# Graph attention layer on one core: the row's largest score kept as one more column of the score tile, both low halves of P written in one VectorE pass, variance plus epsilon on GpSimd

## The chip, the core and the metric

One Trainium2 chip, one of its cores. The metric is the device time of one execution in microseconds (us). Short names as in the profile: PE is TensorE (PEld its weight loads), DVE is VectorE, ACT is ScalarE, POOL is GpSimd, SP is SyncE.

## The reference

`x` is (8, 2048, 256) in f32, `adj` is (8, 2048, 2048) in int32 with about one entry in 512 set, `W` is 256 x 256, `a` has 512 entries.

```python
h = jnp.maximum(_layernorm(x, axis=-1), 0.0)
Wh = jnp.einsum('bnf,fo->bno', h, W)
f1 = Wh @ a[:fout, 0];  f2 = Wh @ a[fout:, 0]
e = f1[:, :, None] + f2[:, None, :]
e = jnp.where(e >= 0, e, ALPHA * e)
attention = jnp.where(adj > 0, e, MASK_FILL)
attention = jax.nn.softmax(attention, axis=1)
h_prime = jnp.einsum('bij,bjo->bio', attention, Wh)
out = x + jax.nn.elu(h_prime)
```

The softmax runs over the rows i. So the kernel holds P transposed: a tile has 128 columns j of the attention on its partitions and all 2048 rows i along the free axis, and a row of that tile is one softmax.

## The kernel before

The work is cut into 128 chunks, 16 for each of the 8 batches; a chunk is 128 nodes j. Each engine has its own program, written out by hand as a loop over steps s, and the programs meet at semaphores. In step s the engines work on these chunks:

- PE: the product h W of chunk s+17 (`make_wh`, L365); `store_block(s-9)`, 24 matmuls for a 128-row block of the upper half of i over the 8 chunks of a group (L435 to L437); `transpose_mask(s+1)`, 16 transposes that put the mask into PSUM (L387); `transpose_x(s+18)` (L377); `direct_blocks(s-1)`, 16 matmuls with the high part of P (L453, L455) and, behind a wait for the low part, 8 with it (L460).
- ACT: `take_f` and `split_v_high` for chunk s+17 (L508, L512), `attention(s)` (L519 to L530), `make_h(s+18)` (L542), at times `keep_part` (L558) and `finish_relu` (L575), `normalise(s+19)` (L548), at times `finish_exp` (L579), and `split_high_stored(s)` (L536), which waits for POOL's 1/total (`inv`).
- DVE: `mask_scores(s)` (L696) adds mask and f1 and takes the largest score of each row in the same pass; `statistics` and `aggregate` of chunk s+23 (L661, L666); every fourth step `add_eps` (L672); `split_v_low(s+17)` (L702); `split_low(s-1)`, two passes of 1024 columns (L710 for the half that is used directly, L715 for the stored half); every fourth step `make_offset` (L677); `make_mask(s+2)` (L684); at times `finish_elu` (L731) and `add_halves` (L726).
- POOL: `split_high(s-1)` (L802, L805, L808); at times the DMA of `finish_add` (L828); every second step the mask load (L794); every fourth step `root`, which makes 1/sqrt(variance + epsilon) of four chunks (L815).

P is written as the sum of two f16 tiles, high and low, for a matmul at f16 speed that keeps more bits; the low one is P minus the high one. `attention(s)` is a chain: Prelu of the largest score (L519, 128x1), Prelu of the score tile (L521, 128x2048), the negated largest as the shift (L523), Exp with that shift as its bias (L530).

The steps with a `root`, called root steps below, are s = 0, 4, 8, ..., 104 (five more lie before step 0). In a root step DVE's order is: scores, statistics, add_eps, v_low, the two low passes, offset, mask, elu, halves, and then the scores of the next step. `make_offset` waits for `root`; everything behind it on DVE waits too, the scores of the next step among it, which ACT's `attention` needs.

Of the kernel before, what the change touches and what calls it, by code (L numbers as in the profile page):

```python
# [13 lines left out]
P = 128  # L14
ALPHA = 0.2
# [6 lines left out]
def graph_attention(nc, x, adj, W, a, out):  # L22
# [27 lines left out]
    with ExitStack() as ctx:  # L50
# [34 lines left out]
        spare = stored[:, 1].rearrange("p g h c -> p (g h c)").bitcast(F32).rearrange("p (i c) -> p i c", c=F)  # L85
# [10 lines left out]
        top = sb("top", [P, R], F32)  # L96
        most = sb("most", [P, R], F32)
# [40 lines left out]
        most_s = sem("most_s")  # L138
# [7 lines left out]
        lo_direct = sem("lo_direct")  # L146
        lo_stored = sem("lo_stored")
# [32 lines left out]
        def f2_col(c):  # L180
            return 64 + c % RF

# [173 lines left out]
        def _(pe):  # L356
# [58 lines left out]
            def store_block(n):  # L415
                group, q = divmod(n, G)
                pe.wait_ge(lo_stored, G * (group + 1))
# [13 lines left out]
                for c in range(G):  # L431
                    p_st = stored[:, group % 2, c]
                    v_c = v[:, (G * group + c) % RV]
                    rows = slice(q * P, (q + 1) * P)
                    nc.tensor.matmul(bank[:, 0:FO], p_st[:, 0, rows], v_c[:, 0, :], start=(c == 0), stop=False)  # L435
                    nc.tensor.matmul(bank[:, 0:FO], p_st[:, 0, rows], v_c[:, 1, :], start=False, stop=False)  # L436
                    last = nc.tensor.matmul(bank[:, 0:FO], p_st[:, 1, rows], v_c[:, 0, :], start=False,  # L437
                                            stop=(c == G - 1))
                last.then_inc(stored_done, 1)

            def direct_blocks(c):
# [5 lines left out]
                p_d = direct[:, c % 2]  # L447
                v_c = v[:, c % RV]
                for m in range(NB):
# [3 lines left out]
                    nc.tensor.matmul(acc[:, m, :], p_d[:, 0, rows], v_c[:, 0, :],  # L453
                                     start=(j == 0 and m % 2 == 0), stop=False, skip_group_check=True)
                    nc.tensor.matmul(acc[:, m, :], p_d[:, 0, rows], v_c[:, 1, :],  # L455
                                     start=False, stop=False, skip_group_check=True)
                pe.wait_ge(lo_direct, c + 1)
                for m in range(NB):
                    rows = slice(m * P, (m + 1) * P)
                    last = nc.tensor.matmul(acc[:, m, :], p_d[:, 1, rows], v_c[:, 0, :],  # L460
# [32 lines left out]
        def _(act):  # L493
# [20 lines left out]
            def attention(c):  # L514
                b, j = divmod(c, C)
                act.wait_ge(scores, c + 1)
                p = prob[:, c % 2, :]
# [9 lines left out]
                act.wait_ge(leaky, c + 1)  # L527
# [5 lines left out]
            def split_high_stored(c):  # L533
                act.wait_ge(inv_ready, c + 1)
                wait(act, stored_done, G * (c // G - 1))
                nc.scalar.activation(stored[:, c // G % 2, c % G, 0, :], prob[:, c % 2, HALF:N], ACT.Copy,  # L536
# [79 lines left out]
        def _(dve):  # L616
# [70 lines left out]
            def mask_scores(c):  # L687
# [4 lines left out]
                if c == 0:  # L692
                    dve.wait_ge(f1_last, 1)
                wait(dve, lo_stored, c - 1)
                wait(dve, most_s, c - R + 1)
                nc.vector.tensor_tensor_reduce(  # L696
                    out=prob[:, c % 2, :], in0=tp_b, in1=f1_row[:, b % 2, :], scale=1.0, scalar=-3.0e38,
                    op0=ALU.add, op1=ALU.max, accum_out=top[:, c % R:c % R + 1]).then_inc(scores, 1)
# [6 lines left out]
            def split_low(c):  # L705
                p = prob[:, c % 2, :]
# [27 lines left out]
            for s in range(FIRST, END + 2):  # L734
                if chunk(s):
                    mask_scores(s)
                for c in measured_at(s):
                    statistics(c)
                    aggregate(c)
                    if c % 4 == 3:  # L740
                        add_eps(c // 4)
# [123 lines left out]
```

## Time and profile before

| | |
|---|---|
| median of 3 runs | 1006.8 us (1006.44 to 1007.97) |
| profiled execution: its time, its span | 1006.23 us, 1004.4 us |
| busy share of the span: PE, ACT, DVE, POOL | 95%, 93%, 87%, 54% |
| granted TensorE clock, mean | 0.997 |
| a batch of 16 chunks, first scores to first scores (503.12 to 621.96) | 118.8 us, that is 7.4 us a step |

A busy share sums the spans of instructions. On ACT and DVE the next instruction starts about 0.1 us before the one in front has ended, so times of a sequence are read from start to start.

### The profile page before, as it was taken

The page shows a single profiled execution, that of the slowest core. Times are in us where ns is not written, and L with a number is a line of the kernel's source. Part 1 is how long each engine was busy: PE and PEld are TensorE (multiplying, and loading weights), DVE is VectorE, ACT ScalarE, POOL GpSimd, SP SyncE. Part 2 cuts the span into 40 slices and gives each one's busy share as a digit, 9 for nine tenths or more (in the row PEclk, how much of TensorE's full clock was granted, in tenths as well). Part 3 has the DMA queues.
Part 4 walks back from the last instruction along what each step waited for, and adds up shares of the span by engine and source line. Part 5 has one row for each costly group of instructions (what it writes and reads, how often), then busy time and mean ns, then how long its engine had stood idle before and what let it go on. Part 6 is the DMA issues. An engine that isn't in the chain of part 4 may idle for free. (4 is left out here: it accounts for less than half of the span.)

```text
span 1004.4 us, 23981 instructions
## 1 busy us (share of the span) xinstructions
PE 958.5 (95%) x8988; PEld 835.2 (83%) x8988; DVE 875.3 (87%) x1261; ACT 929.5 (93%) x1472; POOL 544.0 (54%) x574
## 2 busy tenths in 40 slices
PE   8878999999999999999999999999999999999996
PEld 6656888898888888888888888888888888888886
DVE  7799988999899998899988998899988988798763
ACT  3799999999999999999999999999999999998983
POOL 5445543655545655655556565465565554555534
PEclk9999999999999999999999999999999999999999
DMA  9577657889969978888978987888996987889535
GB/s 222 89 100 116 99 100 119 153 152 161 165 115 164 166 141 157 134 160 158 168 132 137 168 156 148 140 152 152 160 168 114 163 148 125 160 116 147 96 73 168
DMA packets 199061, 142.13 MB, mean 142 GB/s; under 512 B 7329, under 2 KB 187809, under 8 KB 198946
## 3 DMA queue, kind: packets, MB, share of 16 engines
q0 software_dynamic: 140160, 81.80, 60.4%
q1 hardware_dynamic: 58786, 58.81, 19.6%
q8 instruction: 72, 1.18, 0.5%
q14 instruction: 43, 0.35, 0.1%
HBM read 176.16 MB, written 16.84 MB: 192 GB/s over the span
## 5 line engine op out<-in xcount | busy, mean ns | idle before, releaser
L696 DVE CUSTOM_DVE_ANT_0 prob<-tp,f_row 128x2048 f32<-128x2048 bf16 x128 | 292.1, 2282 | 10.5 <-DMA f_row<-f_scratch 10.5
L435 PE MATMUL acc_st<-v,stored 128*128 128x256 f16 x992 | 270.2, 272 | 9.2 <-ACT part L558 5.1
L437 PE MATMUL acc_st<-v,stored 128*128 128x256 f16 x992 | 270.3, 273 | 0.0
L436 PE MATMUL acc_st<-v,stored 128*128 128x256 f16 x992 | 270.3, 272 | 0.0
L530 ACT ACTIVATE prob<-prob,shift 128x2048 f32<-128x2048 f32 x128 | 256.5, 2004 | 9.9
L521 ACT ACTIVATE prob<-prob,f 128x2048 f32<-128x2048 f32 x128 | 255.6, 1997 | 0.0
L808 POOL TENSOR_TENSOR direct<-prob,inv 128x1024 f16<-128x1024 f32 x128 | 242.4, 1894 | 10.0
L802 POOL TENSOR_SCALAR small_total<-total 128x1 f32<-128x1 f32 x128 | 28.7, 224 | 401.9 <-ACT prob L530 401.9
L453 PE MATMUL acc<-v,direct 128*128 128x256 f16 x1024 | 231.4, 273 | 4.8 <-ACT z_direct L564 4.8
L455 PE MATMUL acc<-v,direct 128*128 128x256 f16 x1024 | 231.3, 273 | 0.0
L710 DVE SCALAR_TENSOR_TENSOR direct<-prob,inv,direct 128x1024 f16<-128x1024 f32 x128 | 163.1, 1274 | 23.3 <-POOL direct L808 22.3
L715 DVE SCALAR_TENSOR_TENSOR stored<-prob,inv,stored 128x1024 f16<-128x1024 f32 x128 | 163.6, 1278 | 0.0
L536 ACT ACTIVATE stored<-prob,inv 128x1024 f16<-128x1024 f32 x128 | 146.2, 1142 | 17.0 <-POOL inv L805 17.0
L387 PE MATMUL tp<-ident_b,neg 128*128 128x128 bf16 x2048 | 136.1, 220 | 1.9 <-DVE top L696 1.1
L365 PE MATMUL pre<-w_cat,h_t 128*128 128x258 f32 x444 | 120.9, 394 | 14.7 <-ACT h_t L542 14.6
L460 PE MATMUL acc<-v,direct 128*128 128x256 f16 x1024 | 132.7, 273 | 0.0
L387 PEld LDWEIGHTS tp<-ident_b,neg 128*128 128x128 bf16 x2048 | 125.3, 98 | 7.8 <-issue 5.1
L435 PEld LDWEIGHTS acc_st<-v,stored 128*128 128x128 f16 x992 | 96.8, 98 | 27.6 <-issue 14.9
L436 PEld LDWEIGHTS acc_st<-v,stored 128*128 128x128 f16 x992 | 96.9, 98 | 21.5
L453 PEld LDWEIGHTS acc<-v,direct 128*128 128x128 f16 x1024 | 100.3, 98 | 16.9 <-ACT z_direct L564 6.7
L455 PEld LDWEIGHTS acc<-v,direct 128*128 128x128 f16 x1024 | 100.3, 98 | 11.5
L460 PEld LDWEIGHTS acc<-v,direct 128*128 128x128 f16 x1024 | 100.2, 98 | 11.6
(85 smaller groups left out, 1344.6 us busy)
## 6 DMA issues: line engine op xcount, KB each, us to landing
raw<-in_adj POOLq DMA_DIRECT2D x64, 1024.0 KB, 10.0
y<-in_x SPq DMA_DIRECT2D x64, 256.0 KB, 2.9
out<-y SPq DMA_DIRECT2D x64, 256.0 KB, 2.2
y<-elu POOLq DMA_DIRECT2D x56, 256.0 KB, 4.3
x_in<-in_x SPq DMA_DIRECT2D x108, 128.0 KB, 3.7
f_row<-f_scratch SPq DMA_DIRECT2D x31, 256.0 KB, 6.4
stored<-in_x SPq DMA_DIRECT2D x4, 512.0 KB, 5.9
f_scratch<-f_t SPq DMA_DIRECT2D x124, 0.5 KB
```

The lines of the kernel that those rows point to most:

```text
L387: last = nc.tensor.transpose(tp_b[:, m * P:(m + 1) * P], neg[:, c % 2, m, :], ident_b[:])
L435: nc.tensor.matmul(bank[:, 0:FO], p_st[:, 0, rows], v_c[:, 0, :], start=(c == 0), stop=False)
L436: nc.tensor.matmul(bank[:, 0:FO], p_st[:, 0, rows], v_c[:, 1, :], start=False, stop=False)
L437: last = nc.tensor.matmul(bank[:, 0:FO], p_st[:, 1, rows], v_c[:, 0, :], start=False, stop=(c == G - 1))
L453: nc.tensor.matmul(acc[:, m, :], p_d[:, 0, rows], v_c[:, 0, :], start=(j == 0 and m % 2 == 0), stop=False, skip_group_check=True)
L455: nc.tensor.matmul(acc[:, m, :], p_d[:, 0, rows], v_c[:, 1, :], start=False, stop=False, skip_group_check=True)
L460: last = nc.tensor.matmul(acc[:, m, :], p_d[:, 1, rows], v_c[:, 0, :], start=False, stop=(j == C - 1), skip_group_check=True)
L521: nc.scalar.activation(p, p, ACT.Prelu, bias=f2, alpha=ALPHA).then_inc(leaky, 1)
L530: nc.scalar.activation(p, p, ACT.Exp, bias=shift[:, c % R:c % R + 1], accum_out=total[:, c % R:c % R + 1]).then_inc(prob_ready, 1)
L696: nc.vector.tensor_tensor_reduce(out=prob[:, c % 2, :], in0=tp_b, in1=f1_row[:, b % 2, :], scale=1.0, scalar=-3.0e38, op0=ALU.add, op1=ALU ...
L715: nc.vector.scalar_tensor_tensor(out=st[:, 1, :], in0=p[:, HALF:N], scalar=k, in1=st[:, 0, :], op0=ALU.mult, op1=ALU.subtract).then_inc(lo ...
L808: nc.gpsimd.tensor_tensor(direct[:, c % 2, 0, :], p[:, 0:HALF], k.to_broadcast([P, HALF]), ALU.mult).then_inc(hi_direct, 1)
```

## The change

1. `prob` gets two more columns. `mask_scores` writes the largest score into column 2048 of the score tile, and one Prelu of 2049 columns takes the place of the Prelu of the largest score and that of the tile. The shift now waits for that large Prelu (semaphore `leaky`) and reads its last column.
2. The tiles `direct` and `stored` become slots of one tile `split`, laid out so that the two low halves of a chunk are a pair of slots with a constant step between them. `split_low` is one pass of 128x2x1024, which waits for both high halves and signals `lo_ready`; both readers on PE wait for that.
3. `add_eps` leaves DVE. Its `tensor_scalar` is issued by POOL in `root`, in front of the power.

```diff
-        prob = sb("prob", [P, 2, N], F32)
-        direct = sb("direct", [P, 2, 2, HALF], F16)
-        stored = sb("stored", [P, 2, G, 2, HALF], F16)
+        prob = sb("prob", [P, 2, N + 2], F32)
+        split = sb("split", [P, 4 + 4 * G, HALF], F16)
...
+        def direct_slot(c, low):
+            return (10, 0)[c % 2] + low
+
+        def stored_slot(c, low):
+            return ((12, 2), (28, 20))[c // G % 2][c % 2] + 2 * (c % G // 2) + low
...
-                pe.wait_ge(lo_direct, c + 1)
+                pe.wait_ge(lo_ready, c + 1)
...
-                nc.scalar.activation(most[:, c % R:c % R + 1], top[:, c % R:c % R + 1], ACT.Prelu, bias=f2, alpha=ALPHA
-                                     ).then_inc(most_s, 1)
-                nc.scalar.activation(p, p, ACT.Prelu, bias=f2, alpha=ALPHA).then_inc(leaky, 1)
-                act.wait_ge(most_s, c + 1)
-                nc.scalar.activation(shift[:, c % R:c % R + 1], most[:, c % R:c % R + 1], ACT.Copy, scale=-1.0
+                nc.scalar.activation(p_top, p_top, ACT.Prelu, bias=f2, alpha=ALPHA).then_inc(leaky, 1)
+                act.wait_ge(leaky, c + 1)
+                nc.scalar.activation(shift[:, c % R:c % R + 1], prob[:, c % 2, N:N + 1], ACT.Copy, scale=-1.0
                                      ).then_inc(shift_s, 1)
...
-            def add_eps(g):
-                dve.wait_ge(mv_s, 4 * g + 4)
-                wait(dve, rstd_s, g - RS // 4 + 1)
-                rs = slice(4 * g % RS, 4 * g % RS + 4)
-                nc.vector.tensor_scalar(var_eps[:, rs], mv[:, rs, 1], EPS, None, ALU.add).then_inc(var_s, 1)
...
-                    op0=ALU.add, op1=ALU.max, accum_out=top[:, c % R:c % R + 1]).then_inc(scores, 1)
+                    op0=ALU.add, op1=ALU.max, accum_out=prob[:, c % 2, N:N + 1]).then_inc(scores, 1)
...
                 dve.wait_ge(hi_direct, c + 1)
+                dve.wait_ge(hi_stored, c + 1)
                 wait(dve, direct_done, c - 1)
-                nc.vector.scalar_tensor_tensor(out=direct[:, c % 2, 1, :], in0=p[:, 0:HALF], scalar=k,
-                                               in1=direct[:, c % 2, 0, :], op0=ALU.mult, op1=ALU.subtract
-                                               ).then_inc(lo_direct, 1)
-                dve.wait_ge(hi_stored, c + 1)
-                st = stored[:, c // G % 2, c % G]
-                nc.vector.scalar_tensor_tensor(out=st[:, 1, :], in0=p[:, HALF:N], scalar=k, in1=st[:, 0, :],
-                                               op0=ALU.mult, op1=ALU.subtract).then_inc(lo_stored, 1)
+                nc.vector.scalar_tensor_tensor(
+                    out=split[:, lo_d:lo_s + 1:lo_s - lo_d, :], in0=prob[:, c % 2, 0:N].rearrange("p (h c) -> p h c", h=2),
+                    scalar=inv[:, c % R:c % R + 1], in1=split[:, hi_d:hi_s + 1:hi_s - hi_d, :],
+                    op0=ALU.mult, op1=ALU.subtract).then_inc(lo_ready, 1)
...
             def root(g):
+                rs = slice(4 * g % RS, 4 * g % RS + 4)
+                pool.wait_ge(mv_s, 4 * g + 4)
+                wait(pool, xn_ready, 4 * g + 4 - RS)
+                nc.gpsimd.tensor_scalar(var_eps[:, rs], mv[:, rs, 1], EPS, None, ALU.add).then_inc(var_s, 1)
                 pool.wait_ge(var_s, g + 1)
-                wait(pool, xn_ready, 4 * g + 4 - RS)
-                rs = slice(4 * g % RS, 4 * g % RS + 4)
                 nc.gpsimd.tensor_tensor(rstd[:, rs], var_eps[:, rs], minus_half[:], ALU.pow).then_inc(rstd_s, 1)
```

DVE in root step 72, before, from the statistics on:

```order
L661 BN_STATS stats<-x_in 128x6 [waits mv_s,x_in_s3]
L666 BN_AGGR mv<-stats 128x2 [waits xn_ready,stats_s]
L672 TENSOR_SCALAR var_eps<-mv 128x4 [waits rstd_s,mv_s]
L702 TENSOR_TENSOR v<-pre,v 128x256 [waits v_hi]
L710 SCALAR_TENSOR_TENSOR direct<-prob,inv,direct 128x1024 [waits direct_done,hi_direct]
L715 SCALAR_TENSOR_TENSOR stored<-prob,inv,stored 128x1024 [waits hi_stored]
L677 SCALAR_TENSOR_TENSOR offset<-mv,rstd 128x4 [waits rstd_s]
L684 TENSOR_SCALAR neg<-raw 128x2048 [waits tp_ready,raw_in1]
```

The same place of the changed kernel:

```order
L662 BN_STATS stats<-x_in 128x6 [waits mv_s,x_in_s3]
L667 BN_AGGR mv<-stats 128x2 [waits xn_ready,stats_s]
L696 TENSOR_TENSOR v<-pre,v 128x256 [waits v_hi]
L705 SCALAR_TENSOR_TENSOR split<-prob,inv,split 128x2x1024 [waits direct_done,hi_stored,hi_direct]
L672 SCALAR_TENSOR_TENSOR offset<-mv,rstd 128x4 [waits rstd_s]
L679 TENSOR_SCALAR neg<-raw 128x2048 [waits tp_ready,raw_in1]
```

The variance row is gone and one pass stands where two stood; between the v row and the offset DVE has one instruction of twice the size.

POOL in the same step, before, with the first row of the next step:

```order
L805 TENSOR_TENSOR inv<-small_total,minus_one 128x1 [waits lo_stored,total_s]
L808 TENSOR_TENSOR direct<-prob,inv 128x1024 [waits direct_done,inv_ready]
L794 DMA raw<-in_adj 128x16x256 [waits neg_ready]
L815 TENSOR_TENSOR rstd<-var_eps,minus_half 128x4 [waits xn_ready,var_s]
L802 TENSOR_SCALAR small_total<-total 128x1 [waits prob_ready]
```

The same place of the changed kernel:

```order
L795 TENSOR_TENSOR inv<-small_total,minus_one 128x1 [waits lo_ready,total_s]
L798 TENSOR_TENSOR split<-prob,inv 128x1024 [waits direct_done,inv_ready]
L784 DMA raw<-in_adj 128x16x256 [waits neg_ready]
L805 TENSOR_SCALAR var_eps<-mv 128x4 [waits xn_ready,mv_s]
L807 TENSOR_TENSOR rstd<-var_eps,minus_half 128x4 [waits var_s]
L792 TENSOR_SCALAR small_total<-total 128x1 [waits prob_ready]
```

The variance row now stands behind the mask load's DMA issue and ahead of the power, which waits for it.

## Rows read from the trace of the kernel before

**Rows 1.** Busy time of the engines in one stretch (windows): PE, PEld, DVE, ACT, POOL.

```profile
540.00:660.00 120.00, 118.65 (x1130) 104.31 (x1128) 109.04 (x158) 116.82 (x187) 67.67 (x69) 1.00 0.86 151
```

**Rows 2.** Waits of the whole execution: total us, times, longest us.

```profile
ACT stored L536 <- POOL inv L805: 17.0, 42, 1.0
PE pre L365 <- ACT h_t L542: 14.6, 22, 2.9
ACT most L519 <- DVE top L696: 6.5, 11, 0.7
```

**Rows 3.** Timeline of ACT, step 72 into step 73: start us, duration us, instruction.

```profile
566.48 0.30 ACT L519 ACTIVATE most<-top,f 128x1 f32<-128x1 f32 x1
566.68 1.99 ACT L521 ACTIVATE prob<-prob,f 128x2048 f32<-128x2048 f32 x1
568.58 0.20 ACT L523 ACTIVATE shift<-most 128x1 f32<-128x1 f32 x1
568.85 2.00 ACT L530 ACTIVATE prob<-prob,shift 128x2048 f32<-128x2048 f32 x1
...
573.34 0.29 ACT L519 ACTIVATE most<-top,f 128x1 f32<-128x1 f32 x1
```

**Rows 4.** Timeline of ACT in step 117: the second waits for the first.

```profile
901.78 0.61 ACT L575 ACTIVATE elu<-z_st 128x512 f32<-128x512 f32 x1
902.42 0.63 ACT L579 ACTIVATE elu<-elu 128x512 f32<-128x512 f32 x1
```

**Rows 5.** Groups of instructions by line.

```profile
L805 POOL TENSOR_TENSOR inv<-small_total,minus_one 128x1 f32<-128x1 f32 x128 | 74.6, 583 | 10.8
...
L460 PE MATMUL acc<-v,direct 128*128 128x256 f16 x1024 | 132.7, 273 | 0.0
```

**Rows 6.** Timeline of DVE, root step 72 to the scores of chunk 73.

```profile
566.96 1.28 DVE L710 SCALAR_TENSOR_TENSOR direct<-prob,inv,direct 128x1024 f16<-128x1024 f32 x1
568.15 1.28 DVE L715 SCALAR_TENSOR_TENSOR stored<-prob,inv,stored 128x1024 f16<-128x1024 f32 x1
569.35 0.15 DVE L677 SCALAR_TENSOR_TENSOR offset<-mv,rstd 128x4 f32<-128x4 f32 x1
...
571.02 2.28 DVE L696 CUSTOM_DVE_ANT_0 prob<-tp,f_row 128x2048 f32<-128x2048 bf16 x1
```

**Rows 7.** Timelines of POOL and DVE: the power of root steps 72, 32 and 68.

```profile
567.62 1.53 POOL L815 TENSOR_TENSOR rstd<-var_eps,minus_half 128x4 f32<-128x4 f32 x1
...
268.67 1.05 POOL L815 TENSOR_TENSOR rstd<-var_eps,minus_half 128x4 f32<-128x4 f32 x1 [0.45 <-DVE var_eps L672]
268.82 1.27 DVE L710 SCALAR_TENSOR_TENSOR direct<-prob,inv,direct 128x1024 f16<-128x1024 f32 x1
...
538.35 1.28 DVE L715 SCALAR_TENSOR_TENSOR stored<-prob,inv,stored 128x1024 f16<-128x1024 f32 x1
538.40 2.13 POOL L815 TENSOR_TENSOR rstd<-var_eps,minus_half 128x4 f32<-128x4 f32 x1
540.56 0.16 DVE L677 SCALAR_TENSOR_TENSOR offset<-mv,rstd 128x4 f32<-128x4 f32 x1 [0.94 <-POOL rstd L815]
```

**Rows 8.** Timelines of DVE and POOL, end of root step 68: elu pass, small power.

```profile
541.23 0.23 POOL L802 TENSOR_SCALAR small_total<-total 128x1 f32<-128x1 f32 x1 [0.70 <-ACT prob L530]
541.25 0.70 DVE L731 SCALAR_TENSOR_TENSOR elu<-elu,z_st 128x512 f32<-128x512 f32 x1
541.54 0.84 POOL L805 TENSOR_TENSOR inv<-small_total,minus_one 128x1 f32<-128x1 f32 x1
```

**Rows 9.** Timelines of DVE and ACT: end of the scores, start of attention; steps 65 and 77.

```profile
512.54 0.08 DVE L696 DVE_READ_ACCUMULATOR2_ANT top<- 128x1 f32 x1
514.01 0.32 ACT L519 ACTIVATE most<-top,f 128x1 f32<-128x1 f32 x1
...
602.27 0.08 DVE L696 DVE_READ_ACCUMULATOR2_ANT top<- 128x1 f32 x1
602.75 0.31 ACT L519 ACTIVATE most<-top,f 128x1 f32<-128x1 f32 x1
```

More of the change, by code:

```diff
@@ L431, in store_block @@
                 for c in range(G):
-                    p_st = stored[:, group % 2, c]
+                    p_hi = split[:, stored_slot(G * group + c, 0), :]
+                    p_lo = split[:, stored_slot(G * group + c, 1), :]
                     v_c = v[:, (G * group + c) % RV]
                     rows = slice(q * P, (q + 1) * P)
-                    nc.tensor.matmul(bank[:, 0:FO], p_st[:, 0, rows], v_c[:, 0, :], start=(c == 0), stop=False)
-                    nc.tensor.matmul(bank[:, 0:FO], p_st[:, 0, rows], v_c[:, 1, :], start=False, stop=False)
-                    last = nc.tensor.matmul(bank[:, 0:FO], p_st[:, 1, rows], v_c[:, 0, :], start=False,
+                    nc.tensor.matmul(bank[:, 0:FO], p_hi[:, rows], v_c[:, 0, :], start=(c == 0), stop=False)
+                    nc.tensor.matmul(bank[:, 0:FO], p_hi[:, rows], v_c[:, 1, :], start=False, stop=False)
+                    last = nc.tensor.matmul(bank[:, 0:FO], p_lo[:, rows], v_c[:, 0, :], start=False,
                                             stop=(c == G - 1))
@@ L446, in direct_blocks @@
                     pe.wait_ge(f_ready, LEAD)
-                p_d = direct[:, c % 2]
+                p_hi, p_lo = split[:, direct_slot(c, 0), :], split[:, direct_slot(c, 1), :]
                 v_c = v[:, c % RV]
@@ L452, in direct_blocks @@
                     rows = slice(m * P, (m + 1) * P)
[L453 removed]
+                    nc.tensor.matmul(acc[:, m, :], p_hi[:, rows], v_c[:, 0, :],
                                      start=(j == 0 and m % 2 == 0), stop=False, skip_group_check=True)
[L455 removed]
+                    nc.tensor.matmul(acc[:, m, :], p_hi[:, rows], v_c[:, 1, :],
                                      start=False, stop=False, skip_group_check=True)
[L457 removed]
+                pe.wait_ge(lo_ready, c + 1)
                 for m in range(NB):
                     rows = slice(m * P, (m + 1) * P)
[L460 removed]
+                    last = nc.tensor.matmul(acc[:, m, :], p_lo[:, rows], v_c[:, 0, :],
                                             start=False, stop=(j == C - 1), skip_group_check=True)
@@ L535, in split_high_stored @@
                 wait(act, stored_done, G * (c // G - 1))
-                nc.scalar.activation(stored[:, c // G % 2, c % G, 0, :], prob[:, c % 2, HALF:N], ACT.Copy,
+                nc.scalar.activation(split[:, stored_slot(c, 0), :], prob[:, c % 2, HALF:N], ACT.Copy,
                                      scale=inv[:, c % R:c % R + 1]).then_inc(hi_stored, 1)
@@ L693, in mask_scores @@
                     dve.wait_ge(f1_last, 1)
-                wait(dve, lo_stored, c - 1)
-                wait(dve, most_s, c - R + 1)
+                wait(dve, lo_ready, c - 1)
                 nc.vector.tensor_tensor_reduce(
-                    out=prob[:, c % 2, :], in0=tp_b, in1=f1_row[:, b % 2, :], scale=1.0, scalar=-3.0e38,
-                    op0=ALU.add, op1=ALU.max, accum_out=top[:, c % R:c % R + 1]).then_inc(scores, 1)
+                    out=prob[:, c % 2, 0:N], in0=tp_b, in1=f1_row[:, b % 2, :], scale=1.0, scalar=-3.0e38,
+                    op0=ALU.add, op1=ALU.max, accum_out=prob[:, c % 2, N:N + 1]).then_inc(scores, 1)
             def split_v_low(c):
@@ L803, in split_high @@
                 pool.wait_ge(total_s, c + 1)
-                wait(pool, lo_stored, c - R + 1)
+                wait(pool, lo_ready, c - R + 1)
                 nc.gpsimd.tensor_tensor(k, t, minus_one[:], ALU.pow).then_inc(inv_ready, 1)
```

23 lines of the change are left out of this document (8 added, 15 removed).

## Prediction, made before the changed kernel ran

> **What bounds the kernel now.** I read the windows first. In a stretch of 120 us in the middle PE is busy for 118.65 us and ACT for 116.82, DVE for 109.04 and POOL for 67.67 [rows 1]. By busy time PE would be the bound and ACT a close second; the shares can't decide it, so the list of waits comes next. It has PE waiting for ACT's h_t at L365 (14.6 us in 22 waits), ACT waiting for POOL's `inv` at L536 (17.0 us, 42 waits) and ACT waiting for DVE's scores at L519 (6.5 us, 11 waits) [rows 2]. In the steady part I find no row where ACT waits for PE. So PE follows ACT, and ACT sets the pace: by its own work, by a loop through POOL (Exp, total, `inv`, L536), and at some steps by the scores. The wait for `inv` is a latency that ACT itself starts, so it shortens with nothing here. The wait for the scores is the one to look at, because the change touches what is queued ahead of the scores on DVE.
>
> The timelines say how near DVE is to being late. In step 73 the scores start at 571.02 and last 2.28 us [rows 6]; they end at 573.30, and ACT starts chunk 73 at 573.34 [rows 3]. The list counts no wait there, but there is no slack either. In step 77 the scores have ended at 602.35 and ACT starts at 602.75: 0.40 us. In step 65 it is 512.62 and 514.01: 1.39 us [rows 9]. As a start 0.03 us behind a release is what an engine needs at best (below), the slacks are 0, 0.37 and 1.36 us. These three, with step 69, follow a root step, and from batch 1 on they recur every 16 chunks: 6 steps like 69, 6 like 73, 6 like 65, and 5 like 77, since the last root step is 104.
>
> **The change part by part.** *ACT, attention.* Before, the small Prelu starts at 566.48 and Exp at 568.85: 2.37 us [rows 3]. After, the large Prelu starts where the small one did and takes 1.99 us (one column more is nothing), then the shift waits for it. What such a wait costs is shown by relu and exp of elu in the tail, where the second waits for the first: 901.78 + 0.61 = 902.39, start at 902.42, a gap of 0.03 [rows 4]. Then the shift, 0.20, and the gap to Exp, 0.07 as now (568.78 to 568.85). Sum 1.99 + 0.03 + 0.20 + 0.07 = 2.29, so 0.08 us saved; I take 0.07. Bounds: with a gap of 0.07 behind the large Prelu too, 0.03 to 0.04; with 0.03 at both places, 0.12. So the removed instruction is mostly not won: its issue was 0.20 us, and the overlap of the shift with the Prelu's end is lost. The saving counts only where ACT's own chain decides. 17 of the 128 chunks lie in the waits priced below, and I leave out ten more for the two ends. 100 x 0.07 = **7.0 us won** (3 to 11).
>
> *DVE, one low pass.* The two passes start 1.19 and end their turn 1.20 us later: 568.15 - 566.96 and 569.35 - 568.15, together 2.39 [rows 6]. No pass of this form and 2048 columns is in the trace. The score pass with as many columns takes 2.28 us, or 2.20 to the next start if the overlap is 0.08 as for the low pass (1.28 against 1.20). Between 2.20 and 2.39 I take 2.25: 0.14 us less. On DVE that is off the path except where DVE is what ACT waits for. The direct low half is ready about 1 us later than now. PE has 16 high-part matmuls in front of the low ones, and in the whole execution no idle time ahead of L460 [rows 5], so I cost it at nothing in the steady part; in the last chunk it may lie bare, at most one half pass, and I leave it out.
>
> *add_eps to POOL.* DVE loses a small instruction whose successor, v_low, waits for ACT's v anyway in most steps: nothing on the path. POOL gets one, 0.23 us as its 128x1 row has, and 0.08 to the next (541.23 + 0.23 to 541.54) [rows 8]: 0.31 us ahead of the power in each root step. Behind the power on POOL is the next chunk's total; behind `make_offset` on DVE are mask, elu, halves and the next scores.
>
> *The two together.* This is the term that decides. The same power (128x4) takes 1.53, 1.05 and 2.13 us [rows 7], and the lengths have a pattern. In step 32 it starts at 268.67, before the first low pass (268.82), and takes 1.05. In step 72 it starts at 567.62, inside the first pass; its end less 1.05 is 569.15 - 1.05 = 568.10, just where the second pass starts (568.15) [rows 6, 7]. In step 68 it starts at 538.40, just inside the second pass, and its end less 1.05 is 539.48; that pass ends at 538.35 + 1.20 = 539.55. So POOL's power seems to stand still until a low pass is over and to slip in at the seam between two. The small power shows the same beside the elu pass: 0.84 us instead of 0.583 [rows 5, 8]. Taking the seam away takes POOL's way in.
>
> The Trainium skill (page "SBUF — State Buffer", section "SBUF: two separate sides") says that VectorE and GpSimd share a port pair that is held "for the whole instruction" by a VectorE operation with two SBUF inputs, against a GpSimd operation that reads SBUF, and that the other blocks fully. By that rule the merge speaks against the change; by a rule of shared bandwidth the power would only be stretched and rival 1 would hold. The lengths above agree with the lock.
>
> With T the start of the low pass, a root step after the change is: POOL gets to the variance at T + 0.66 (567.62 - 566.96), is held until T + 2.25 - 0.05, then 0.23 + 0.08 + 1.05, and the offset follows 0.03 later (as 540.53 to 540.56): T + 3.59. Before, it was T + 2.39. The offset and all behind it are **1.20 us later**. Where POOL comes late, as in step 68, it was T + 3.41 already (540.56 less 538.35 - 1.19), so 0.18 later. The price by kind of step: like 73, no slack, 6 x 1.20 = 7.2; like 77, 5 x (1.20 - 0.37) = 4.2; like 69, 6 x 0.18 = 1.1; like 65, nothing by way of the scores (1.36 of slack). But there DVE's mask and elu passes, 1.2 us later, now lie where POOL makes `inv`. Row 541.54 shows 0.26 us for half a collision; with the mask pass and a whole elu pass (about 0.6 to the next start) it could be 0.8, and ACT's L536 waits for it. I take 0.5: 6 x 0.5 = 3.0 (0 to 4.8). **Lost: 15.5 us.** The same in steps like 73 and 77 hides behind the wait for the scores.
>
> Sum: 1006.2 - 7.0 + 15.5 = 1014.7 us for an execution like the profiled one; the median of the runs is 0.6 above that one's 1006.23, so 1015.3.
>
> **The rivals.**
> 1. *No hold by the pass* (the power slowed in proportion, or let in somewhere inside a pass): the root ends 0.31 later, the offset waits for 569.15 + 0.31 + 0.03 = 569.49 instead of 569.35. Steps like 73 lose 0.14, like 69 0.31, the others nothing: 6 x 0.14 + 6 x 0.31 = 2.7, against 7.0 won: -4.3, 1002.5 us. For it: everything it needs is in single rows. Against it: the three ends at the seams. It decides for faster where the offset comes less than 0.8 us later: 6d + 5(d - 0.37) = 7.0.
> 2. *The hold is there but half hidden.* PE gets time to catch up while ACT waits, POOL may reach the variance before the pass starts in some steps, and ACT may win 0.12 instead of 0.07 a chunk: 11.4 + 1.1 lost, 11 to 12 won: +1, about 1007.5, within 0.2%.
> 3. *ACT wins next to nothing and the collisions are whole:* 11.4 + 1.1 + 4.8 - 3 = +14.3, 1021 us. This is the upper end of my own case, not a case apart.
>
> **How the numbers follow.** My forecast, the hold of a whole pass at its price, 0.74, with its own range 1009.5 to 1021; rival 2 with 0.10; rival 1 with 0.16. 0.2% (2.0 us) is about what a measurement of this kernel can tell from no change. Slower by more than that: the forecast and a little of rival 2, 0.76; faster: 0.15; within: 0.09. The range must leave out no more than 2 in 10: from 1006, which leaves out rival 1, to 1021.
>
> **What the changed profile would show.** One low pass of 2.3 us per chunk. Small instructions on POOL in root steps: the variance row with a long span or a late end, whose end falls just behind the end of the low pass, and a power of 1.05 us behind it, not 1.5 to 2.1. `make_offset` with idle time ahead of it put down to POOL's rstd, about 1.2 us in each root step where it had none. ACT's first Prelu waiting for DVE's scores in 17 more or longer waits, steps like 73 and 77 foremost, and some for `inv` in steps like 64. Large Prelu to Exp, start to start, 2.3 us. No idle time ahead of PE's low-part matmuls. Wrong I would be if the variance row ran inside the low pass in its 0.2 us, or if the wait of the shift for the large Prelu were several tenths dearer or cheaper than 0.03.

## The result, and the profile after

The changed kernel takes 1014.53 us (median of 4 runs, 1014.3 to 1014.78) against 1006.63 us for the kernel before in the same comparison. The ratio is 1.0076, with a 95% interval of 1.0058 to 1.0093: slower, by 7.9 us where 8.5 had been forecast. The profiled execution has a span of 1012.5 us against 1004.4. In the experiments below the ratios leave out executions more than 1.5% above the fastest of their kernel, which are the profiled ones of e1 and e3, at a granted clock of 0.559 and 0.753 (1649.9 and 1232.8 us), for which both kernels were profiled again as e1b and e3b, and two of e9 (1016.5 and 1017.9 us).

The list of waits of the changed kernel (total us, times, longest us) answers to [rows 2]:

```profile
DVE offset L672 <- POOL rstd L807: 33.9, 28, 1.3
...
ACT split L537 <- POOL inv L795: 27.2, 53, 1.0
...
ACT prob L523 <- DVE prob L690: 12.2, 23, 0.7
...
PEld acc L464 <- DVE split L705: 6.1, 14, 0.6
```

The first row is the new one. The offset waited 6.6 us in all before; it now waits 33.9 us, about 1.25 in nearly every root step. ACT's waits for `inv` went from 17.0 to 27.2 us and its waits for the scores from 6.5 to 12.2 (11 waits before, 23 now). The last row had no counterpart before; none of its 14 waits lies between 94 and 888 us, so it belongs to the first and the last steps.

The timelines of root step 72, first DVE, then POOL, then ACT, answer to [rows 3], [rows 6] and [rows 7]:

```profile
571.46 2.34 DVE L705 SCALAR_TENSOR_TENSOR split<-prob,inv,split 128x2048 f16<-128x2048 f32 x1
575.05 0.16 DVE L672 SCALAR_TENSOR_TENSOR offset<-mv,rstd 128x4 f32<-128x4 f32 x1 [1.25 <-POOL rstd L807]
575.14 0.69 DVE L679 TENSOR_SCALAR neg<-raw 128x2048 bf16<-128x2048 bf16 x1
575.75 0.68 DVE L723 SCALAR_TENSOR_TENSOR elu<-elu,z_st 128x512 f32<-128x512 f32 x1
...
576.74 2.28 DVE L690 CUSTOM_DVE_ANT_0 prob<-tp,f_row 128x2048 f32<-128x2048 bf16 x1
```

```profile
572.13 1.76 POOL L805 TENSOR_SCALAR var_eps<-mv 128x4 f32<-128x4 f32 x1
573.97 1.05 POOL L807 TENSOR_TENSOR rstd<-var_eps,minus_half 128x4 f32<-128x4 f32 x1
575.45 0.48 POOL L792 TENSOR_SCALAR small_total<-total 128x1 f32<-128x1 f32 x1 [0.42 <-ACT prob L531]
576.01 0.85 POOL L795 TENSOR_TENSOR inv<-small_total,minus_one 128x1 f32<-128x1 f32 x1
```

```profile
570.98 2.01 ACT L523 ACTIVATE prob<-prob,f 128x2049 f32<-128x2049 f32 x1
573.03 0.20 ACT L525 ACTIVATE shift<-prob 128x1 f32<-128x1 f32 x1
573.26 2.00 ACT L531 ACTIVATE prob<-prob,shift 128x2048 f32<-128x2048 f32 x1
...
576.89 1.15 ACT L537 ACTIVATE split<-prob,inv 128x1024 f16<-128x1024 f32 x1 [0.77 <-POOL inv L795]
...
579.06 2.00 ACT L523 ACTIVATE prob<-prob,f 128x2049 f32<-128x2049 f32 x1 [0.71 <-DVE prob L690]
```

Read it with T = 571.46. The low pass ends its turn at T + 2.26, as steps without a root show, where the next instruction starts that much behind it. The variance row, four numbers per partition, lasts 1.76 us: it is issued at T + 0.67, and its end less 0.23 is 573.66, 0.06 before the end of the pass. Behind it the power takes 1.05 us, no longer 1.53. The offset starts at T + 3.59, to the hundredth what had been reckoned, and the scores of chunk 73 start 1.2 us later against T than in [rows 6]. Both POOL instructions that lie beside the mask and elu passes (0.48 and 0.85 us, where [rows 5] and [rows 8] have 0.58 for the second and 0.23 for the first) are the collision at `inv`. In step 64 they take 0.48 and 0.85 as well, with 0.23 and 0.56 before, and ACT waits 0.41 us for `inv` there: that is the loss of the row r = 0 below.

Where the time went can be read step by step. This table gives the time from one large Prelu to the next on ACT, in us, as the mean over batches 1 to 5, worked out from the starts in the timelines of each profiled execution; r is the step's place in its batch, and the root steps are r = 0, 4, 8, 12. What a root step costs shows in its own row. The columns are the kernel before, the changed one, and the experiments below.

```
 r     before  after   e1b    e2   e3b    e4    e5    e6    e7    e9
 0      7.83   8.26   7.76  8.13  8.06  7.77  8.29  7.82  7.74  8.59
 1      7.65   7.60   7.61  7.61  7.61  7.61  7.60  7.66  7.62  7.60
 4      7.92   8.08   7.90  7.77  8.22  8.19  7.30  6.82  6.79  7.18
 6      6.91   6.75   6.91  6.76  6.89  7.14  6.76  6.91  6.91  6.76
 7      7.50   7.41   7.41  7.42  7.42  7.42  7.42  7.61  7.83  7.41
 8      6.87   8.08   6.86  7.77  7.91  7.50  7.30  6.91  6.98  6.98
12      6.84   7.70   6.75  7.39  7.53  6.75  7.31  6.83  6.75  6.76
14      6.85   6.76   6.77  6.76  6.77  6.77  6.76  6.85  6.77  6.76
batch 119.25 120.82 118.23 119.81 120.55 119.41 118.86 118.35 117.51 118.48
```

After against before: four rows are longer, r = 8 by 1.21, r = 12 by 0.86, r = 0 by 0.43 and r = 4 by 0.16. Of the others r = 6 is 0.16 shorter, r = 1 0.05, the rest 0.08 to 0.10, the win of the column (large Prelu to Exp is 573.26 - 570.98 = 2.28 against 2.37).

### The profile page after: what moved, and what is told of

Its sections match the earlier page's. It is cut to its first block, busy times and chain, and to the rows that moved or that the text cites. A ratio compares the mean times of both kernels' runs of the same rounds, so it can differ in the third digit from the quotient of the medians.

```text
span 1012.5 us, 23687 instructions
## 1 busy us (share of the span) xinstructions
PE 960.8 (95%) x8988; PEld 833.2 (82%) x8988; DVE 846.0 (84%) x1101; ACT 922.3 (91%) x1344; POOL 585.5 (58%) x606
## 4 chain that ended last, share of the span: by engine, by line
POOL 42%; issue 37%; PE 9%; ACT 5%; DVE 3%; DMA 2%; POOLq 1%; SPq 0%; ACTq 0%; DVEq 0%
POOL split L798 15%; POOL raw L784 6%; POOL inv L795 6%; POOL var_eps L805 4%; POOL y L820 4%; POOL rstd L807 3%; ACT prob L523 3%; POOL small_total L792 3%; DVE prob L690 2%; PE pre L368 1%; DMA out<-y 1%; PE acc L464 1%; PE acc_st L439 1%; PE acc_st L441 1%; PE acc_st L440 1%
## 5 line engine op out<-in xcount | busy, mean ns | idle before, releaser
L705 DVE SCALAR_TENSOR_TENSOR split<-prob,inv,split 128x2048 f16<-128x2048 f32 x128 | 299.6, 2341 | 23.7 <-POOL split L798 22.8
L439 PE MATMUL acc_st<-v,split 128*128 128x256 f16 x992 | 270.1, 272 | 6.4 <-ACT part L559 3.7
L441 PE MATMUL acc_st<-v,split 128*128 128x256 f16 x992 | 270.4, 273 | 0.0
L440 PE MATMUL acc_st<-v,split 128*128 128x256 f16 x992 | 270.3, 272 | 0.0
L523 ACT ACTIVATE prob<-prob,f 128x2049 f32<-128x2049 f32 x128 | 257.4, 2011 | 12.3 <-DVE prob L690 12.2
L792 POOL TENSOR_SCALAR small_total<-total 128x1 f32<-128x1 f32 x128 | 36.1, 282 | 367.2 <-ACT prob L531 367.2
L798 POOL TENSOR_TENSOR split<-prob,inv 128x1024 f16<-128x1024 f32 x128 | 242.3, 1893 | 10.0
L457 PE MATMUL acc<-v,split 128*128 128x256 f16 x1024 | 231.6, 273 | 7.5 <-ACT z_direct L565 7.5
L459 PE MATMUL acc<-v,split 128*128 128x256 f16 x1024 | 231.5, 273 | 0.0
L537 ACT ACTIVATE split<-prob,inv 128x1024 f16<-128x1024 f32 x128 | 146.4, 1143 | 27.3 <-POOL inv L795 27.2
L368 PE MATMUL pre<-w_cat,h_t 128*128 128x258 f32 x444 | 121.8, 396 | 16.6 <-ACT h_t L543 16.5
L464 PE MATMUL acc<-v,split 128*128 128x256 f16 x1024 | 132.9, 273 | 2.3 <-DVE split L705 2.2
L439 PEld LDWEIGHTS acc_st<-v,split 128*128 128x128 f16 x992 | 96.7, 98 | 26.6 <-issue 13.8
L457 PEld LDWEIGHTS acc<-v,split 128*128 128x128 f16 x1024 | 100.4, 98 | 19.7 <-ACT z_direct L565 9.4
L440 PEld LDWEIGHTS acc_st<-v,split 128*128 128x128 f16 x992 | 96.8, 98 | 20.8
L464 PEld LDWEIGHTS acc<-v,split 128*128 128x128 f16 x1024 | 99.0, 98 | 17.4 <-DVE split L705 6.1
L459 PEld LDWEIGHTS acc<-v,split 128*128 128x128 f16 x1024 | 100.4, 98 | 11.5
L368 PEld LDWEIGHTS pre<-w_cat,h_t 128*128 128x128 f32 x444 | 76.2, 191 | 37.7 <-ACT h_t L543 29.9
## 6 DMA issues: line engine op xcount, KB each, us to landing
raw<-in_adj POOLq DMA_DIRECT2D x64, 1024.0 KB, 10.2
```

The costliest lines, as they stand in the source:

```text
L439: nc.tensor.matmul(bank[:, 0:FO], p_hi[:, rows], v_c[:, 0, :], start=(c == 0), stop=False)
L440: nc.tensor.matmul(bank[:, 0:FO], p_hi[:, rows], v_c[:, 1, :], start=False, stop=False)
L441: last = nc.tensor.matmul(bank[:, 0:FO], p_lo[:, rows], v_c[:, 0, :], start=False, stop=(c == G - 1))
L457: nc.tensor.matmul(acc[:, m, :], p_hi[:, rows], v_c[:, 0, :], start=(j == 0 and m % 2 == 0), stop=False, skip_group_check=True)
L459: nc.tensor.matmul(acc[:, m, :], p_hi[:, rows], v_c[:, 1, :], start=False, stop=False, skip_group_check=True)
L464: last = nc.tensor.matmul(acc[:, m, :], p_lo[:, rows], v_c[:, 0, :], start=False, stop=(j == C - 1), skip_group_check=True)
```

## The experiments

All medians stand beside the kernel before in the same comparison (1006.9 us for e1 to e4, 1007.4 for e5 to e7 and e1b, 1007.2 for e9 to e11); intervals are of the ratio to it. Two theories are told apart. The hold: a small POOL instruction stands still until VectorE's running low pass is over, so the price lies in how many seams the pass leaves and in who waits for the offset. The rivals: one more POOL instruction by itself, the direct half that comes later for PE, or the longer wait on ACT.

**e1_column_only.** The kernel before with part 1 alone.

```diff
-                nc.scalar.activation(most[:, c % R:c % R + 1], top[:, c % R:c % R + 1], ACT.Prelu, bias=f2, alpha=ALPHA
-                                     ).then_inc(most_s, 1)
-                nc.scalar.activation(p, p, ACT.Prelu, bias=f2, alpha=ALPHA).then_inc(leaky, 1)
...
+                nc.scalar.activation(p_top, p_top, ACT.Prelu, bias=f2, alpha=ALPHA).then_inc(leaky, 1)
```

> The kernel before with part 1 of the change alone (largest score as a column of the score tile; two low passes, add_eps on VectorE). Hold theory: the loss of the whole change lies in the root steps and is made by the single low pass and by the variance row on GpSimd; this part has neither, so it can only win. In the changed kernel's trace large Prelu to Exp is 2.28 us (570.98 to 573.26) against 2.37 before, 0.09 won; about 100 chunks in which ScalarE's own chain decides give 9 us: 998 us (996 to 1001). Rival theory (the wait of the shift for the large Prelu costs what the small Prelu gave, and part of the +8 us lies here): 1006 to 1010 us.

Measured: 1001.2 us, ratio 0.994 (0.9928 to 0.9953). The same kernel, measured and profiled again:

> The kernel of e1_column_only again, for a profile with the clock at its full level. Per step of a batch, large Prelu to large Prelu: 0.09 less than before in most steps, and about the same as before in steps 6 and 8 of the batch, where the scores had no slack before the change: 1000 us as measured, not the 998 that I had reckoned.

Measured: 999.8 us, ratio 0.9923 (0.991 to 0.9936). The column alone wins 6 to 8 us, against 9 expected: the table has no win at r = 6 and r = 8, and 0.02 us at r = 4. There the scores had no slack, and with two passes and add_eps on DVE they are as late as ever. No part of the 8 us lies here.

**e2_merge_eps_on_dve.** The changed kernel with add_eps back on DVE.

> The changed kernel with add_eps back on VectorE: column and single low pass. Hold theory: GpSimd's power, the only instruction in front of the offset, stands still until the low pass that began at T ends (T + 2.2), then 1.05 and 0.03: offset at T + 3.29, 0.90 us later than before, where it was T + 2.39. Steps like 73 lose 6 x 0.90, like 77 5 x (0.90 - 0.37), like 69 win 6 x 0.12, collisions at inv in steps like 65 6 x 0.2; against 9 won by the column: 1006 us (1003 to 1009). The power should last 2.5 to 3.0 us in root steps like 72 and 76 and end at one time behind the end of the low pass. Rival theory (what costs is the 0.31 us of one more GpSimd instruction, not the pass): the power as long as before, 1.5 to 2.1 us, and 997 to 999 us.

Measured: 1008.4 us, ratio 1.002 (1.0011 to 1.0028), 6 us faster than the changed kernel. The timeline of DVE and POOL in root step 72:

```profile
567.83 2.34 DVE L711 SCALAR_TENSOR_TENSOR split<-prob,inv,split 128x2048 f16<-128x2048 f32 x1
...
568.48 2.59 POOL L813 TENSOR_TENSOR rstd<-var_eps,minus_half 128x4 f32<-128x4 f32 x1
...
571.11 0.16 DVE L678 SCALAR_TENSOR_TENSOR offset<-mv,rstd 128x4 f32<-128x4 f32 x1 [0.94 <-POOL rstd L813]
```

The power is now the instruction held: its end less 1.05 is 570.02, 0.07 before the pass ends its turn (567.83 + 2.26). The offset is at T + 3.28 (3.29 expected). The table has +0.90 at r = 8 and +0.55 at r = 12 against before, as reckoned. So the single pass does harm without the variance row on POOL. The median is above the expected 1006 because at r = 0 the collision cost 0.30, not 0.2, and because the column was worth less than 9. The rival asked for a power as short as before and 999 us at most; both fail.

**e3_two_passes.** The changed kernel, low pass in two of 1024 columns, one signal at the end.

```diff
-                nc.vector.scalar_tensor_tensor(
-                    out=split[:, lo_d:lo_s + 1:lo_s - lo_d, :], in0=prob[:, c % 2, 0:N].rearrange("p (h c) -> p h c", h=2),
...
+                for i in range(2):
+                    hi, lo = ((hi_d, lo_d), (hi_s, lo_s))[1024 * i // HALF]
+                    r = 1024 * i % HALF
...
+                last.then_inc(lo_ready, 1)
```

> The changed kernel with the low pass cut in two of 1024 columns again, both signalled once at the end, add_eps on GpSimd. Hold theory: the variance row gets in at the seam (T + 1.14), but the power behind it is 0.3 us too late for it and stands until the second pass ends (T + 2.34), then 1.05 and 0.03: offset at T + 3.42, still 1.03 us later than before. So cutting the pass in two mends little: 1012 us (1009 to 1014). Steps like 73 6 x 1.03, like 77 5 x 0.66, like 69 6 x 0.32, collisions 3, less 9. The variance row should be short or end at the seam, and the power be the long one. Rival theory (one long pass instead of two is what costs, by the late direct half for TensorE or by length alone): the loss goes away, 999 to 1003 us.

Measured: 1012.6 us, ratio 1.006 (1.0047 to 1.0073). The repeated one:

> The kernel of e3_two_passes again, for a profile with the clock at its full level. Hold theory: in steps like 72 the variance row ends just behind the first low pass (about T + 1.4) and the power, issued at T + 1.45, ends 1.05 us behind the second pass, at T + 3.39; 1012 us as measured.

Measured: 1013.1 us in one execution. DVE (both passes in one row) and POOL in root step 72:

```profile
570.43 2.48 DVE L708 SCALAR_TENSOR_TENSOR split<-prob,inv,split 128x1024 f16<-128x1024 f32 x2
...
573.86 0.16 DVE L672 SCALAR_TENSOR_TENSOR offset<-mv,rstd 128x4 f32<-128x4 f32 x1 [0.95 <-POOL rstd L811]
```

```profile
571.10 0.69 POOL L809 TENSOR_SCALAR var_eps<-mv 128x4 f32<-128x4 f32 x1
571.88 1.94 POOL L811 TENSOR_TENSOR rstd<-var_eps,minus_half 128x4 f32<-128x4 f32 x1
```

The variance row ends at T + 1.36, behind the first pass, the power's end less 1.05 is T + 2.34, the end of the second, and the offset is at T + 3.43 (3.42 expected). Splitting the pass again mends only 2 us: in steps like 72 the variance row uses up the one seam, and the power behind it is held by the second pass. Each of parts 2 and 3 alone makes the offset late by 0.9 to 1.0 us, and both together by 1.2. The rival by which one long pass is the whole cause is out: it wanted 999 to 1003 us here. The late direct half is as late here as in the changed kernel, so this run says nothing of it; e9 and e11 do.

**e4_four_passes.** The same with `range(4)` and 512 columns.

> The same as e3_two_passes with four low passes of 512 columns, start to start 0.60, so that VectorE is busy as long and the direct half is signalled as late, but there are three seams. Hold theory: in steps like 76 and 64 GpSimd comes at T + 0.3, gets in at T + 0.55, the power at T + 1.15, done at T + 2.2, no wait of the offset; in steps like 72 (T + 0.66) the power gets in at T + 1.75, offset at T + 2.83, 0.44 late; steps like 68 no later than before. 6 x 0.44 = 2.6 lost, 9 won: 1000 us (998 to 1004), 12 us faster than e3_two_passes though nothing but the number of seams differs. Rival theory (GpSimd is slowed in proportion to VectorE's work, or length and lateness of the low halves cost): the same as e3_two_passes within 2 us.

Measured: 1008.3 us, ratio 1.0012 (1.0003 to 1.0021). That is 4.3 us faster than e3, not 12. The seams work as reckoned (root step 64):

```profile
506.27 2.73 DVE L708 SCALAR_TENSOR_TENSOR split<-prob,inv,split 128x512 f16<-128x512 f32 x4
508.92 0.15 DVE L672 SCALAR_TENSOR_TENSOR offset<-mv,rstd 128x4 f32<-128x4 f32 x1
...
506.58 0.53 POOL L809 TENSOR_SCALAR var_eps<-mv 128x4 f32<-128x4 f32 x1
507.19 1.41 POOL L811 TENSOR_TENSOR rstd<-var_eps,minus_half 128x4 f32<-128x4 f32 x1
```

Both POOL rows are short, and the offset stands right behind the passes with no wait. What failed is a size: four passes take 2.65 us from start to start (506.27 to 508.92), not 2.40. That is 0.26 more than two, in every step, and shows at r = 6 (7.14 against 6.91), in 22 waits of PE's weight loads for the low part (12.8 us; 14 and 6.1 in the changed kernel), and at the end. At r = 12 the loss is gone whole (6.75), at r = 8 it is 0.63, where 0.44 had been reckoned from shorter passes. At r = 4 the offset comes at T + 3.68, not 3.41 as before, and 0.27 us are lost where the expectation had none. The time alone (neither 12 us faster than e3 nor within 2) would leave the question open; the durations answer it.

**e5_late_offset.** The changed kernel, nothing on POOL altered; DVE makes the offset one step later.

```diff
                 if chunk(s):
                     mask_scores(s)
+                if s > 0 and offset_at(s - 1) is not None:
+                    make_offset(offset_at(s - 1))
...
-                if offset_at(s) is not None:
+                if offset_at(s) is not None and s < 0:
```

> The changed kernel with one thing moved: from step 0 on make_offset stands in VectorE's next step, behind the scores, where its first reader (ScalarE's normalise of that step) still comes later. The single low pass and the GpSimd variance stay, so the hold stays. Hold theory: variance and power on GpSimd are held as long as in the changed kernel and end at the same T + 3.55, but nothing of VectorE waits for them: the 1.21 us of steps like 72, 0.86 of 76, 0.16 of 68 and the collision at inv in 64 go, and also the 0.8 that the scores of steps like 69 waited already before the change. 118.8 - 0.8 - 16 x 0.09 = 116.6 us a batch for ScalarE; TensorE without a wait needs 16 x 7.24 = 115.8 and waits about 1.3 at the batch's start, 117.1; so TensorE is nearly the bound: 995 us (992 to 998). Rival theory (the cost is GpSimd's or TensorE's by the late low half, not VectorE's wait for the offset): 1010 us or more.

Measured: 1003.0 us, ratio 0.9958 (0.9946 to 0.997). That is 11.5 us below the changed kernel, but 8 us above the 995 expected, and not all of it is loss of the change taken back: the same move wins 7 us on the kernel before (e6). Row by row, r = 8 and r = 12 had lost 2.07 us together and get 1.17 back; r = 4 gets 0.78, where the kernel before gets 1.10; r = 0 keeps its whole loss (8.29 against 7.83). POOL and DVE in root step 72 tell why:

```profile
565.37 2.32 POOL L807 TENSOR_SCALAR var_eps<-mv 128x4 f32<-128x4 f32 x1
567.77 1.40 POOL L809 TENSOR_TENSOR rstd<-var_eps,minus_half 128x4 f32<-128x4 f32 x1
569.25 0.23 POOL L794 TENSOR_SCALAR small_total<-total 128x1 f32<-128x1 f32 x1
```

```profile
564.71 2.34 DVE L705 SCALAR_TENSOR_TENSOR split<-prob,inv,split 128x2048 f16<-128x2048 f32 x1
566.97 0.69 DVE L679 TENSOR_SCALAR neg<-raw 128x2048 bf16<-128x2048 bf16 x1
567.57 0.69 DVE L723 SCALAR_TENSOR_TENSOR elu<-elu,z_st 128x512 f32<-128x512 f32 x1
...
570.77 1.36 DVE L672 SCALAR_TENSOR_TENSOR offset<-mv,rstd 128x4 f32<-128x4 f32 x1
```

With no idle gap on DVE behind the low pass, the variance row is held through the mask pass too (its end less 0.23 is 567.46, just before that pass ends its turn at 567.57), and the power through the elu pass (569.17 - 1.05 = 568.12). My expectation had both end at T + 3.55; they end at T + 4.46. The total of the next chunk, queued behind them on POOL, starts at 569.25 though Exp's accumulator was out at 568.60, and ACT waits 0.82 us for `inv` there. A part of the wait did not go; it moved to the other queue.

**e6_before_late_offset.** That move on the kernel before.

> The kernel before with that one move alone. Hold theory: only the wait of steps like 68 is taken away (0.8 us for ScalarE, 6 times): 1002 us (1000 to 1004). Rival theory (the wait of the offset before the change cost nothing): 1006 to 1007 us.

Measured: 1000.4 us, ratio 0.9933 (0.9921 to 0.9945). Row r = 4 is 1.10 shorter than before: the wait of the offset in steps like 68 ([rows 7], 0.94 us) was on the path already.

**e7_column_late_offset.** Column and late offset; two passes and add_eps on DVE as before.

> Column and late offset, with two low passes and add_eps on VectorE as before. Against e5_late_offset this prices the single pass and the GpSimd variance where nobody waits for the offset. Hold theory: then both parts are off the path but for 0.14 us of VectorE time a step: within 2 us of e5_late_offset, 995 to 998 us.

Measured: 993.1 us, ratio 0.9861 (0.9848 to 0.9874), the fastest kernel of all, 14.3 us (1.4%) below the kernel before. It is 10 us faster than e5 and not within 2, so parts 2 and 3 cost that much even when nothing on DVE waits for the offset. The traces agree where nothing else disturbs them: batch 2 takes 118.88 us in e5 and 116.89 in e7, the four root rows giving 2.13 and r = 6 taking 0.13 back. That 0.13 is what the shorter low pass is worth where the scores have no slack: r = 6 takes 6.75 with one pass, 6.88 with two.

The row r = 7 of e7 is a mean of unlike steps: 7.41 or 7.42 in three batches, 8.41 and 8.48 in batches 1 and 5. DVE and POOL in step 87 show where these come from:

```profile
669.77 0.43 DVE L655 BATCH_NORM_STATS2 stats<-x_in 128x6 f32<-128x256 f32 x1 [1.93 <-DMA x_in<-in_x]
...
672.33 1.42 POOL L797 TENSOR_SCALAR small_total<-total 128x1 f32<-128x1 f32 x1 [3.14 <-ACT prob L524]
```

DVE stands 1.93 us for the input tile of its statistics, everything behind it comes later, and the low passes now lie beside POOL's total, which takes 1.42 us and not 0.23. From batch 1 on, no such wait is in the kernel before, the changed one, e1b to e5; e6 has one, e7 two, and the three kernels below four to six each. Why the tile comes late there no run isolates.

**e9_root_first.** The whole change, with `root` issued directly behind `split_high` on POOL, before both DMAs.

```diff
                     split_high(s - 1)
+                if s >= 0 and root_at(s) is not None:
+                    root(root_at(s))
                 for k in finish(s - 2):
...
-                if root_at(s) is not None:
+                if s < 0 and root_at(s) is not None:
                     root(root_at(s))
```

> The whole change, with one thing moved on GpSimd: from step 0 on, root (variance and power) is issued directly behind split_high, ahead of the DMAs of finish_add and of the mask load. Hold theory: GpSimd then comes to them before the low pass starts: about 0.6 us before T in steps like 72 (mask load's 1.27 ahead of it in the changed kernel, T + 0.67), 1.0 before in 64 and 76, 0.6 before in 68. The variance row takes 0.23, the power 1.05 (as in step 32 of the kernel before, where it began 0.15 ahead of the pass), and the offset waits for nothing. All of the change's losses go (1.21, 0.86, 0.43 and 0.16 a batch), and the wait of 0.8 in steps like 69: 995 us (993 to 999). Rival theory (merge or GpSimd variance cost by themselves, wherever they stand): above 1003 us. The mask load is issued 1.4 us later every fourth step; if that mattered, VectorE's mask pass would wait for its DMA.

Measured: 1003.9 us (12 runs, 999.1 to 1017.9), ratio 0.9962 (0.9941 to 0.9982). The expectation of 995 is missed by 9 us, and by time alone the rival's mark of 1003 is reached. The rows decide. Two root steps of its profiled execution, 76 and 72, POOL and DVE of each:

```profile
591.56 0.23 POOL L805 TENSOR_SCALAR var_eps<-mv 128x4 f32<-128x4 f32 x1
591.88 1.05 POOL L807 TENSOR_TENSOR rstd<-var_eps,minus_half 128x4 f32<-128x4 f32 x1
592.53 2.34 DVE L705 SCALAR_TENSOR_TENSOR split<-prob,inv,split 128x2048 f16<-128x2048 f32 x1
...
562.44 2.34 DVE L705 SCALAR_TENSOR_TENSOR split<-prob,inv,split 128x2048 f16<-128x2048 f32 x1
...
562.30 0.24 POOL L805 TENSOR_SCALAR var_eps<-mv 128x4 f32<-128x4 f32 x1 [0.53 <-DVE mv L667]
562.63 3.06 POOL L807 TENSOR_TENSOR rstd<-var_eps,minus_half 128x4 f32<-128x4 f32 x1
```

The first is the expected one: 0.23 and 1.05 us ahead of the pass, and no loss. The second shows what I missed: where POOL waits for the statistics (0.53 us), the power starts 0.19 us behind the start of the pass and is held for all of it, 3.06 us. That happened in 4 of the 22 root steps from step 20 on (48, 64, 72, 80). So one execution prices the hold against itself: the step of 72 takes 7.90 us, the same place of the other batches 6.74 or 6.75; the steps of 48, 64 and 80 take 8.68, 8.68 and 8.93, those of 32 and 96, where nothing was held, 7.76 and 7.75. This is the clearest test of the hold, since the kernel is the same and what differs inside these steps is the order of two starts.

The held steps go with late transfers. In front of 48, 64 and 80 DVE's scores had waited 1.59, 1.47 and 3.46 us for `f_row`, in front of 32 and 96 only 1.10 and 0.80; in front of 72 the statistics of step 71 had waited 0.86 us for `x_in` (though those of 67 waited 1.08, and the power of 68 got in 0.08 us ahead of the pass). The longest of these waits also makes one step of 9.36 us, which is the 8.10 of row r = 15. That such waits, with an order of starts that tenths of a microsecond turn, make the runs spread over 19 us is a reading that no run isolates.

**e10_before_root_first** and **e11_column_root_first** make the same move on the kernel before and on column alone.

> The kernel before with that move alone. The power starts ahead of the low pass and takes 1.05 us; only steps like 69 win (0.8 us each, 6 times), as the move of the offset in e6_before_late_offset showed with 1000.4: 1000 to 1002 us.

> Column and root first, two low passes and add_eps on VectorE. Against e9_root_first it prices the single low pass and the GpSimd variance where nothing is held: VectorE 0.14 us a step longer, which shows in steps like 71 and 73, where the scores have no slack: 994 us, from 1 us faster to 3 us slower than e9_root_first.

Measured: 1005.0 us (ratio 0.9982, 0.9969 to 0.9995) and 997.8 us (0.9911, 0.9894 to 0.9929). e10 wins 2 us, less than the 5 to 7 expected: its batch is 118.84 against 119.25, r = 4 is 0.94 shorter, but r = 7 and r = 8 are 0.39 and 0.17 longer. Of DVE's six waits for `x_in` (0.41 to 2.95 us) four lie at r = 7, and the 7.89 of that row is one step of 9.50 among four of 7.49; batch 2, which has no such wait, takes 118.19 against 119.15. e11 is 6 us faster than e9 by medians, outside what was expected (from 1 faster to 3 slower); the spread of e9 allows no closer reading of the times. Batch 2 does: there nothing is held in e9 and no tile comes late in either, and e9 takes 117.02 us, e11 117.20. So where nothing is held, the single pass, the late half and the variance row on POOL cost nothing, and the shorter pass even wins its 0.13 at r = 6 (6.75 against 6.88). This is the rival that e3 could not settle. e7 remains the best.

## Why the prediction was right

Each step of it against what was measured:

- **ACT sets the pace.** Not contradicted: ACT's waits for the scores and for `inv` grew by 5.7 and 10.2 us (12 and 11 more of them, where 17 more or longer ones had been named for the scores), and PE's waits for h_t hardly moved (14.6 to 16.5 us). ACT's step times take in the whole loss, but they would do so whichever engine set the pace, so they do not prove it.
- **The column saves 0.07 us a chunk** (bounds 0.03 to 0.12). 0.09 in the trace: the wait behind the large Prelu cost 0.04 (570.98 + 2.01 to 573.03) and the gap to Exp was 0.03, where I had 0.03 and 0.07.
- **The low pass at 2.25 us.** 2.26.
- **Held by the pass: offset at T + 3.59, 1.20 later.** 3.59. Steps like 73: 1.21 measured, 1.20 reckoned. Like 77: 0.86 and 0.83. Like 69: 0.16 and 0.18. Like 65, by the collision at `inv`: 0.43 and 0.5. Together 6 x 1.21 + 5 x 0.86 + 6 x 0.16 + 6 x 0.43 = 15.1 us against 15.5.
- **The low half later for PE at nothing.** In the steady part just so: no wait between 94 and 888 us. In the last chunk it lay bare, as had been allowed and left out: the last low pass starts at 979.77, and PE's low-part matmuls wait 0.36 us for it (982.18), with nothing behind which to hide.
- **The sum.** +8.5 reckoned, +8.1 in the span of the profiled execution and +7.9 in the medians. In the span, the first large Prelu comes 0.4 us earlier, the 127 steps from ACT's first large Prelu to its last take 7.4 longer, and what is behind it 1.1. The 7.4 are the 15.1 above less 7.7 for the column and the small rest, where I had 7.0. That the larger win and the end's loss nearly cancel was luck.

So the mechanism was the forecast one. In the 26 root steps of the changed kernel from step 4 on, the instruction that meets the low pass (the variance row, in step 32 the power) ends, less its bare length, 0.13 to 0.16 us before the recorded end of the pass, which is 0.05 to 0.08 before the pass ends its turn.

The Trainium skill's rule ("SBUF — State Buffer", "SBUF: two separate sides") that a VectorE operation with two SBUF inputs blocks a GpSimd one that reads SBUF for its whole length is borne out by these rows and by those of e2, e3b, e4 and e9. The same sentence of the page lets whichever starts first block the other. The traces do not agree for a small GpSimd operation that starts first: the power of step 76 in e9 runs from 591.88 to 592.93, and the pass that starts inside it, at 592.53, still takes 2.34 us; in [rows 7] a pass started 0.15 us behind the power takes 1.27. Of the rivals, the first is refuted by these rows (the power at 3.06 us in e9, 1.05 in the same kernel 29 us later), the second by the table.

What I did not see is how much the kernel before already lost in steps like 68, and that the hold can reach ACT a second way, by POOL's own queue; both came out in e5 to e7.

## What to carry to other kernels

Before merging two VectorE passes with two SBUF inputs, look at what GpSimd does beside them: a seam between passes can be the only moment at which its small instructions get in, and a merge that saves 0.14 us can cost 1.2. A small instruction moved to an idle GpSimd is not free if it comes to stand beside such passes: look at its end, not its length, and at what is queued behind it. And put an instruction that waits for another engine (here the offset) behind the work that the critical engine is waiting for; that one move was worth 7 us alone. When a row of a table of means stands out, look at the single steps before explaining it: one late tile in two batches made the 7.83 of e7.

## What the runs showed that I had not expected

- The seam between the low pass and the mask pass (a bf16 `tensor_scalar`, 0.60 us from start to start) let nothing in: in e5 the variance row waited through both, 2.32 us. The seam between two low passes did let it in (e3b, 0.69 us), and so did the one between the mask and the elu pass.
- The score pass, whose mask comes from PSUM, held nothing: in the kernel before it runs from 510.33 to 512.54, and POOL's total and `inv` of step 64, at 510.74 and 511.05 inside it, take their bare 0.23 and 0.56 us.
- A long POOL instruction can hold a VectorE one. In e5 VectorE's offset, 128x4, lasts 1.36 us (570.77 to 572.13), until POOL's 128x1024 product ends (570.22 + 1.89 = 572.11); in the changed kernel it lasts 0.16.
- Cutting a pass costs: two of 1024 take 2.39 us of VectorE's time, one of 2048 takes 2.26, four of 512 take 2.65.
- An instruction on ACT that waits for the one in front of it on the same engine starts 0.03 to 0.04 us behind its end; the overlap of 0.1 us that it forgoes is the larger part of what the wait costs.
